# Batch 0's head in a four-batch chain of conditional layers: first expert piece by chunk, a new load order, and sums placed in other units

## What is computed

```python
def _gemma_mlp(x, gate_w, up_w, down_w):          # width 256 -> 1024 -> 256
    g = jnp.einsum('bsh,hi->bsi', x, gate_w)
    u = jnp.einsum('bsh,hi->bsi', x, up_w)
    return jnp.einsum('bsi,ih->bsh', jax.nn.gelu(g, approximate=True) * u, down_w)

x = x + top2_of_8_experts(x, softmax(cond)) + _gemma_mlp(x, shared...)       # L0
x = x + (silu(x @ W_up[e] + b_up[e]) * (x @ W_gate[e] + b_gate[e])) @ W_down[e] + b_down[e]   # L1, e = argmax(cond)
x = x + x @ sum_g(cond[g] * weight[g] * mask).T + bias                       # L2, masked
x = x + x @ W_base.T + b_base + 2 * sum_e cond[e] * (x @ As[e].T) @ Bs[e].T  # L3, rank 16
```

## Time and profile before

| what | value |
|---|---|
| median of 3 runs | 494.46 us (492.17 to 495.14) |
| the profiled execution | 492.72 us |
| its span, first to last instruction | 491.1 us |
| TensorE busy | 476.2 us, 97% |
| VectorE busy | 398.1 us, 81% |
| ScalarE busy | 274.6 us, 56% |
| GpSimd busy | 89.4 us, 18% |
| TensorE's granted clock | 1.00 throughout |

### The profile page before, as it was taken

The page is one execution under the profiler, slowest core; times in us unless marked ns, Lnnn a source line. Parts: engine busy times, 40 slices in busy tenths (PEclk is TensorE's granted clock), DMA queues, the critical chain, the costliest instruction groups (busy, mean ns, idle before and its releaser), DMA issues.

```text
span 491.1 us, 6836 instructions
## 1 busy us (share of the span) xinstructions
PE 476.2 (97%) x2166; PEld 393.8 (80%) x2166; DVE 398.1 (81%) x679; ACT 274.6 (56%) x448; POOL 89.4 (18%) x92
## 2 busy tenths in 40 slices
PE   8899888989999999999999999999999999999997
PEld 7688666768888888888888888888888888888886
DVE  7589988999878787578987979898887799974455
ACT  5556554666645565356654746675766356544432
POOL 1913239900009950100000020000000100000000
PEclk9999999999999999999999999999999999999999
DMA  6978773040931106872293016213039423000002
GB/s 173 204 223 249 142 113 116 1 128 29 194 115 41 32 5 135 179 209 75 70 171 81 1 48 188 77 53 111 20 86 185 118 64 102 28 1 1 0 1 85
DMA packets 112363, 47.33 MB, mean 96 GB/s; under 512 B 66424, under 2 KB 111096, under 8 KB 112328
## 3 DMA queue, kind: packets, MB, share of 16 engines
q1 hardware_dynamic: 109184, 41.30, 34.2%
q0 software_dynamic: 2560, 5.21, 4.3%
q10 hardware_dynamic: 584, 0.39, 0.3%
HBM read 44.79 MB, written 2.10 MB: 95 GB/s over the span
## 4 chain that ended last, share of the span: by engine, by line
PE 82%; DVE 8%; SPq 5%; DMA 3%; issue 1%; ACT 0%; ACTq 0%; DVEq 0%
PE bank_a L1671 7%; PE bank_b L1673 7%; PE bank_b L1671 7%; PE bank_a L1673 7%; PE bank_a L1672 7%; PE bank_b L1672 7%; PE tail L1695 4%; PE tail L1696 4%; PE tail L1699 4%; SPq L496 3%; PE out L1699 3%; PE out L1695 3%; PE out L1696 3%; PE bank_a L1938 2%; PE bank_a L1940 2%; PE bank_a L1939 2%
## 5 line engine op out<-in xcount | busy, mean ns | idle before, releaser
L713 ACT ACTIVATE hid_hi<-hid 128x512 fp32r<-128x512 f32 x84 | 53.1, 632 | 84.8 <-DVE hid L1006 53.8
L1014 DVE TENSOR_TENSOR hid_lo<-hid,hid_hi 128x512 fp32r<-128x512 f32 x84 | 61.9, 737 | 18.4 <-ACT hid_hi L713 18.4
L1006 DVE SCALAR_TENSOR_TENSOR hid<-bank_b,mine,hid 128x512 f32<-128x512 f32 x64 | 47.5, 742 | 27.8 <-PE bank_b L1673 26.7
L705 ACT ACTIVATE hid<-bank_a 128x512 f32<-128x512 f32 x68 | 40.4, 594 | 40.9 <-PE bank_a L1673 40.0
L995 DVE TENSOR_TENSOR res_lo<-raw,res_hi 128x768 fp32r<-128x768 f32 x36 | 36.1, 1004 | 1.1 <-ACT res_hi L692 1.1
L995 DVE TENSOR_TENSOR w_lo<-raw,w_hi 128x768 fp32r<-128x768 f32 x30 | 29.5, 984 | 2.8 <-ACT w_hi L692 2.8
L692 ACT ACTIVATE res_hi<-raw 128x768 fp32r<-128x768 f32 x36 | 30.2, 839 | 1.2 <-DMA raw<-in_L_cond_skill_down 1.2
L1671 PE MATMUL bank_a<-x_hi,res_hi 128*128 128x512 f32 x74 | 28.9, 390 | 0.0
L1672 PE MATMUL bank_a<-x_lo,res_hi 128*128 128x512 f32 x74 | 28.8, 390 | 0.0
L1673 PE MATMUL bank_a<-x_hi,res_lo 128*128 128x512 f32 x74 | 28.8, 389 | 0.0
L1671 PE MATMUL bank_b<-x_hi,res_hi 128*128 128x512 f32 x74 | 28.8, 389 | 0.0
(11 more groups left out here) (362 smaller groups left out, 1349.8 us busy)
## 6 DMA issues: line engine op xcount, KB each, us to landing
raw<-in_L_cond_skill_gate SPq DMA_DIRECT2D x32, 256.0 KB, 3.2
raw<-in_L_cond_skill_up SPq DMA_DIRECT2D x32, 256.0 KB, 3.4
raw<-in_L_cond_skill_down SPq DMA_DIRECT2D x64, 128.0 KB, 3.5
raw<-in_L_cond_shared_down SPq DMA_DIRECT2D x18, 128.0 KB, 3.7
early<-in_L_cond_weight POOLq DMA_DIRECT2D x2, 1024.0 KB, 7.1
raw<-in_L_cond_shared_gate SPq DMA_DIRECT2D x8, 256.0 KB, 3.4
raw<-in_L_cond_shared_up SPq DMA_DIRECT2D x8, 256.0 KB, 3.6
raw_gate<-in_L_cond_W_gate SPq DMA_DIRECT2D x16, 128.0 KB, 4.0
```

Of the source, the lines that this page charges most:

```text
L705: nc.scalar.activation(hid[:, tile_of(g)], bank_a[tile_of(g)][:, :], func, **kw).then_inc(act_ready, 1)
L713: nc.scalar.activation(hid_hi[:, tile_of(g)], hid[:, tile_of(g)], ACT.Copy).then_inc(hid_hi_ready, 1)
L1006: ins = nc.vector.scalar_tensor_tensor(tile, bank, weight, tile, ALU.mult, ALU.mult)
L1014: nc.vector.tensor_tensor(hid_lo[:, tile], hid[:, tile], hid_hi[:, tile].bitcast(F32), ALU.subtract).then_inc(hid_lo_ready, 1)
```

## The change

- Piece 1 (the first expert's first two chunks) is loaded by chunk: three transfers for a chunk (gate, up, down) on a semaphore of its own, six in all in place of four. ScalarE's `split` waits for the chunk alone. `take_chosen` moves ahead of `first_parts`' first subtraction.
- `PIECE_ORDER` of batch 0: joint pieces 2, 4 and 6 each one or two places earlier; L1's 12 transfers behind own piece 12, not 14.
- `first_combined`'s parts go from units 5, 7, 9, 10 to 2, 5, 7, 9; ScalarE's part of them from 8 and 9 to 6 and 8; `pair_main_hi` and `pair_sums` from 10 to 9, `pair_main_lo` from 11 to 10, c3's sum from 9 to 10 and its high part from 10 to 11.
- `bias_base` goes from joint unit 0 to batch 1's unit 1, `bias_lora` from there to unit 3.
- `share` becomes b3_t (256 columns), and `first_a2` multiplies and adds in halves of 256 columns: 14 pairs in place of 7 for each of the two batches. It waits for l3_f in place of base_sums.

```diff
--- before.py
+++ after.py
@@ -58,10 +58,10 @@
 L3_LO_AT = 8
 W2_AT = 8
 BIAS_LOADS_AT = 11
-T_AT = {5: 0, 7: 1, 9: 2, 10: 3}
-T_HI_AT = {8: ((0, 2), (2, 3)), 9: ((1, 4), (3, 5))}
-MAIN_AT = 10
-SUMS_AT = {0: 10, 2: 4}
+T_AT = {2: 0, 5: 1, 7: 2, 9: 3}
+T_HI_AT = {6: ((0, 2), (2, 3), (1, 4)), 8: ((3, 5),)}
+MAIN_AT = 9
+SUMS_AT = {0: 9, 2: 4}
 SUMS_LO_AT = {0: 11, 2: 5}
 
 C_PLACE = {0: 9, 1: 11, 2: 1, 3: 3}
@@ -75,7 +75,8 @@
 X2_SUM = {1: 5, 2: 5}
 X2_PLACE = {1: 5, 2: 4}
 XSUM_SECOND = 12
-BIAS_LORA_AT = 1
+BIAS_BASE_AT = 1
+BIAS_LORA_AT = 3
 BIAS_AT = 3
 L1_TURN = {13: 0, 14: 1, 15: 2, 16: 3}
 L1_TURN_LO = {14: 0, 15: 1, 16: 2, 17: 3}
@@ -146,7 +147,8 @@
     return (i - (SHARED if b < JOINT else 0)) // MLP_CHUNKS
 
 
-PIECE_ORDER = ([("own", 0, c) for c in range(0, 14, 2)] + [("joint", 0, 2), ("own", 0, 14), ("joint", 0, 4), ("own", 0, 16), ("joint", 0, 6)]
+PIECE_ORDER = ([("own", 0, c) for c in range(0, 10, 2)] + [("joint", 0, 2), ("own", 0, 10), ("own", 0, 12), ("joint", 0, 4), ("own", 0, 14),
+                ("joint", 0, 6), ("own", 0, 16)]
                + [("own", 1, c) for c in range(0, OWN[1], 2)]
                + [("own", 2, 0), ("own", 2, 2), ("own", 2, 4), ("joint", 2, 0), ("own", 2, 6), ("own", 2, 8), ("joint", 2, 2),
                   ("own", 2, 10), ("joint", 2, 4), ("own", 2, 12), ("joint", 2, 6), ("own", 2, 14)]
@@ -162,7 +164,7 @@
 
 
 def raw_landed(j):
-    return 64 * ((j - 1) // RAW_SLOTS + 1)
+    return 64 * ((j - 1) // RAW_SLOTS + (raw_slot(j) > 0))
 
 
 SLOTS = [[i % 4 if i < UNIT_AT[0] else i % 2 for i in range(OWN[0])],
@@ -230,6 +232,7 @@
         a3_lo = sb("a3_lo", [P, D], F32R)
         b3_raw = raw_down1[:, 1, :]
         b3_t = sb("b3_t", [P, D])
+        share = b3_t[:, :]
         b3_y = raw_up1[:, :, :].rearrange("p k h -> p (k h)")
         b3_y_hi = sb("b3_y_hi", [P, B * D], F32R)
         b3_y_lo = sb("b3_y_lo", [P, B * D], F32R)
@@ -243,7 +246,6 @@
         u3_work = raw_down1[:, 3, :]
         bias_all = sb("bias_all", [P, B, D])
         base_nat = sb("base_nat", [P, KD, D])[:, :, :]
-        share = base_nat.rearrange("p k d -> p (k d)")
         b3_nat = bias_all[:, 0, :].rearrange("p (k e r) -> p k e r", k=KD, e=E)
         bias2_again = bias_all[:, 1, :]
         b3_u3 = bias_all[:, 2, :].rearrange("p (k e r) -> p k e r", k=KD, e=E)
@@ -299,6 +301,7 @@
 
         raw_in = [sem(f"raw_in{s}") for s in range(RAW_SLOTS)]
         second_in = sem("second_in")
+        skill_in = [sem(f"skill_in{c}") for c in range(2)]
         first_down_in = [sem(f"first_down_in{c}") for c in range(2)]
         x0_in = [sem(f"x0_in{k}") for k in range(KD)]
         x_in = [None] + [sem(f"x_in{b}") for b in range(1, B)]
@@ -352,6 +355,7 @@
         xs_lo_ready = sem("xs_lo_ready")
         a2_step = sem("a2_step")
         a2_share = sem("a2_share")
+        a2_sum = sem("a2_sum")
         weights_f = sem("weights_f")
         weights_hi = sem("weights_hi")
         weights_lo = sem("weights_lo")
@@ -474,6 +478,8 @@
                         sp.wait_ge(pair_w_lo, PARTS * (PAIRED[b2] + c2 + 1 - FIRST_JOINT[b2]) + 2)
                 m = c if kind == "joint" or (b < JOINT and c < SHARED) else (c - (SHARED if b < JOINT else 0)) % MLP_CHUNKS
                 cols = slice(m * P, (m + 2) * P)
+                if j == 1:
+                    return load_by_chunk(slot, m, gate, up, down)
                 for n, w in ((0, gate), (2, up)):
                     sp.dma_start(raw[:, slot, n:n + 2, :],
                                  w.rearrange("(k p) i -> p k i", p=P)[:, :, cols]).then_inc(raw_in[slot], 16)
@@ -481,6 +487,15 @@
                     sp.dma_start(raw[:, slot, 4:6, half_n * P:(half_n + 1) * P],
                                  down[(m + half_n) * P:(m + half_n + 1) * P, :]
                                  .rearrange("p (j d) -> p j d", j=KD)).then_inc(raw_in[slot], 16)
+
+            def load_by_chunk(slot, m, gate, up, down):
+
+                for c in range(2):
+                    place, rows = slice(c * P, (c + 1) * P), slice((m + c) * P, (m + c + 1) * P)
+                    for n, w in ((0, gate), (2, up)):
+                        sp.dma_start(raw[:, slot, n:n + 2, place],
+                                     w.rearrange("(k p) i -> p k i", p=P)[:, :, rows]).then_inc(skill_in[c], 16)
+                    sp.dma_start(raw[:, slot, 4:6, place], down[rows, :].rearrange("p (j d) -> p j d", j=KD)).then_inc(skill_in[c], 16)
 
             shared = [t["L0_cond_shared_" + n] for n in ("gate", "up", "down")]
             skill = [t["L0_cond_skill_" + n] for n in ("gate", "up", "down")]
@@ -548,7 +563,7 @@
                 load_piece(j, *(rows if kind == "own" and own_skill >= 0 else shared))
                 if (kind, b, c) == ("own", 0, 4):
                     load_x(1)
-                if (kind, b, c) == ("own", 0, 14):
+                if (kind, b, c) == ("own", 0, 12):
                     for n in range(3):
                         first_l1(n)
                 if (kind, b, c) == ("own", 1, 2):
@@ -609,17 +624,20 @@
             def first_a2(b):
 
                 if b == 0:
-                    pool.wait_ge(base_sums, KD)
+                    pool.wait_ge(l3_f, 1)
                     pool.wait_ge(w2_in, 48)
                     pool.wait_ge(tail_free, len(PREPS))
                 else:
                     pool.wait_ge(weights_lo, 3 * b - 1)
                 nc.gpsimd.tensor_scalar(a2[:, :], w2_raw[:, 0, :], picks[:, b, 5:6], None, ALU.mult).then_inc(a2_step, 1)
                 for n in range(1, E):
-                    pool.wait_ge(a2_step, b * A_STEPS + n)
-                    nc.gpsimd.tensor_scalar(share, w2_raw[:, n, :], picks[:, b, 5 + n:6 + n], None, ALU.mult).then_inc(a2_share, 1)
-                    pool.wait_ge(a2_share, b * (E - 1) + n)
-                    nc.gpsimd.tensor_tensor(a2[:, :], a2[:, :], share, ALU.add).then_inc(a2_step, 1)
+                    for k in range(KD):
+                        part, done = slice(k * D, (k + 1) * D), b * (E - 1) + n - 1
+                        pool.wait_ge(a2_step, b * A_STEPS + n)
+                        wait(pool, a2_sum, done + k)
+                        nc.gpsimd.tensor_scalar(share, w2_raw[:, n, part], picks[:, b, 5 + n:6 + n], None, ALU.mult).then_inc(a2_share, 1)
+                        pool.wait_ge(a2_share, KD * done + k + 1)
+                        nc.gpsimd.tensor_tensor(a2[:, part], a2[:, part], share, ALU.add).then_inc((a2_sum, a2_step)[k], 1)
                 pool.wait_ge(a2_step, b * A_STEPS + E)
                 nc.gpsimd.tensor_tensor(a2[:, :], a2[:, :], mask_nat[:, :], ALU.mult).then_inc(a2_step, 1)
                 pool.wait_ge(a2_step, b * A_STEPS + E + 1)
@@ -673,7 +691,10 @@
         def _(act):
             def split(b, i):
                 j = piece_of("own", b, i)
-                act.wait_ge(raw_in[raw_slot(j)], raw_landed(j))
+                if j == 1:
+                    act.wait_ge(skill_in[i % 2], 48)
+                else:
+                    act.wait_ge(raw_in[raw_slot(j)], raw_landed(j))
                 earlier = slot_before(b, i)
                 if earlier is not None:
                     act.wait_ge(down_done, downs_done(*earlier))
@@ -881,12 +902,12 @@
                         l3_operand_hi()
                     if i in T_HI_AT:
                         combined_hi(0, T_HI_AT[i])
-                    if i == C_PLACE[0] + 1:
-                        weights_split_hi(c3_hi, c3[:, :], (weights_f, 1))
                     if i == MAIN_AT:
                         pair_main_hi(0, 0)
                     if i == SUMS_AT[0] + 1:
                         pair_sums_hi(0, 0)
+                    if i == SUMS_LO_AT[0]:
+                        weights_split_hi(c3_hi, c3[:, :], (weights_f, 1))
 
             def second():
                 b = 1
@@ -1338,6 +1359,8 @@
                         x_turn_blocks(1)
                     if i == X1_LO_AT:
                         later_x_lo(1)
+                    if i in T_AT:
+                        first_combined(T_AT[i])
                     if i == L3_TURN_AT:
                         l3_turn_blocks()
                     if i == L3_OPERAND_AT:
@@ -1345,17 +1368,13 @@
                         l3_operand()
                     if i == L3_LO_AT:
                         l3_operand_lo()
-                    if i in T_AT:
-                        first_combined(T_AT[i])
-                    if i == C_PLACE[0]:
-                        c3_sum(0)
                     if i == SUMS_AT[0]:
                         pair_sums(0, 0)
                     if i == MAIN_AT + 1:
                         pair_main_lo(0, 0)
+                        c3_sum(0)
                     if i == SUMS_LO_AT[0]:
                         pair_sums_lo(0, 0)
-                    if i == C_PLACE[0] + 2:
                         weights_split_lo(0, 1, c3_hi, c3_lo, c3[:, :])
 
             def first_combined(part):
@@ -1407,6 +1426,8 @@
                         residual_lo(b, 1)
```

(7 more changed lines are left out.)

## The result

| | before | after |
|---|---|---|
| median (lowest to highest), 15 runs each | 493.56 us (491.04 to 496.32) | 489.75 us (488.53 to 493.25) |
| ratio, 95% interval | | 0.9932 (0.991 to 0.9955) |
| the profiled execution, its span | 492.72, 491.1 us | 492.13, 490.2 us |

The change is worth 3.8 us (0.8%; by the ratio, 3.4 us), where I had forecast 7.0; so it falls under "within 1%". The profiled execution of the changed kernel is one of its longer ones. The first experiment therefore profiled the same kernel again.

The account below looks back on a forecast made before the run. TensorE is full from 120 us on, so only its earlier waits, 10.6 us at most, can go. 2.0 + 1.9 + 1.5 + 0.6 + 1.5 - 0.5 = 7.0 us, from 494.46 to 487.5 us; range 484.2 to 491.2.

Parts of the forecast that it names:

- Part 1 (A): 2.3 us TensorE wait at 13.6 us for the first expert's first weights; loading by chunk takes away 2.0 us.
- F: 1.9 us TensorE wait on L1533 at 98.6 us; kept as it is in the forecast.
- Part 2 (B): 1.9 us wait at 57.7 us for joint unit 0's low part; spreading the sums takes it all away.
- Part 3 (C): 1.6 us wait at 69.8 us for VectorE's sum; moving bias_base out of joint unit 0 gains 1.5 us.
- Part 4 (D, F): GpSimd's sum in halves, started sooner: holds of 0.55 us, not 1.1; 0.6 us gained, 0.5 us subtracted for longer overlap.
- D: 1.2 us TensorE wait at 73.2 us for VectorE's hid_lo, held by GpSimd; 0.6 us taken as gone.
- Part 5 (E): 1.5 us wait at 77.9 us on ScalarE's copy; joint piece 4 issued near 61 us removes it, 3 us slack.
- VectorE gives it back: Rival, chance 0.20: joint units 1 to 4 become VectorE-bound through holding, giving back 3.5 us; 491.0.
- joint piece 4 is still late: Rival, chance 0.10: L1's 12 transfers need 24 us beside GpSimd's loads; about 1.5 us of wait stays; 489.0.
- slower case through long holds: Rival, chance 0.05: halves hold VectorE as long as wholes in joint units 0 to 3; TensorE waits 10 us more; 497.
- three signs of being wrong: Two-input VectorE instructions held 1.1 us; SyncE's L1 issues past 65 us; hid_lo or L1533 waits summing over 4 us.

Follow-up runs that it names:

- after_again: The changed kernel, unaltered, timed and profiled again beside the kernel before: 489.23 us, ratio 0.992.
- l1_up_behind_joint4: The changed kernel with the last four of L1's 12 transfers issued behind joint piece 4, not in front of it: 487.84 us, ratio 0.9893.
- the base: The changed kernel with the last four of L1's 12 transfers issued behind own piece 14: 487.19 us, ratio 0.9864.
- the four of the second group: Against the base: a2's additions made one-input multiplications 485.49, batch 0's a2 in wholes 487.08, a2 from joint unit 4 487.03, bias_base in joint unit 0 488.29 us.
- whole_sums: The base with a2 of batch 0 summed in wholes of 512 columns on another, more coarsely rounded tile: 487.08 us, ratio 0.9889.
- sums_as_before: The base with block sums, weight sums, joint weights' parts and c3 in the units of the kernel before: 489.58 us, ratio 0.9917.
- piece1_whole: The base with piece 1 loaded whole again by four transfers, take_chosen still early: 488.02 us, ratio 0.9885.
- c0_at_10: The base with the product that needs b3_y_lo one unit later, in unit 10: 486.17 us, ratio 0.9855.
- one_input_adds: The base with GpSimd's a2 additions replaced by one-input multiplications, leaving out the sum over eight weights: 485.49 us, ratio 0.9845.
- best: c0_at_10 plus batch 0's a2 from joint unit 4, its split in batch 1's unit 2, bias columns' stores before batch 1's a2: 483.50 us, ratio 0.9792.
- order_as_before: The changed kernel with PIECE_ORDER and the place of L1's transfers as in the kernel before: 493.51 us, ratio 0.9999.

## Why the prediction was half right

**Part 1 (A): right in its place, wrong in what it is worth.** The third transfer was issued at 8.33 us in after_again (forecast 8.4), ScalarE had its data by 11.1 (11.9), TensorE began unit 2 at 13.42 (13.8): 2.4 us sooner than before. The failed sentence is "whatever TensorE gains before that moves the whole rest forward by as much". It holds only where VectorE isn't the bound, and the rows that I had read said it was: 9.96 of 10 us busy from 40 to 50 us, beside a full TensorE. The other failed sentence is "I cost the later pieces at nothing". VectorE's timeline of after_again:

```profile
27.42 0.96 DVE L1016 TENSOR_TENSOR w_lo<-raw,w_hi 128x768 fp32r<-128x768 f32 x1 [1.30 <-ACT w_hi L713]
...
46.74 1.22 DVE L1304 TENSOR_TENSOR b_y_lo<-raw_up,b_y_hi 128x1024 fp32r<-128x1024 f32 x1
```

At 27.4 us VectorE had stood idle for 1.30 us, because ScalarE had waited 2.5 us for the next piece to land; from there to 50 us it has no pause of over 0.4 us. So b3_y_lo comes at 46.74 where it was 46.48 before, although TensorE started unit 2 2.4 us earlier. Seven profiles have this same head without slow first products (after_again, l1_up_behind_joint4, the base and the four of the second group). The split that waits for this landing starts at 26.38 to 28.12 us in them, b3_y_lo 19.0 to 19.3 us behind it in each, and at 50 us TensorE is 1.80 us (earliest landing, whole_sums) to 0.06 us (latest, the base) ahead of the kernel before. So the landing and VectorE's list behind it set this place, and what is left of A differs from execution to execution. With the sums in their old units (sums_as_before) the same stretch of VectorE takes 18.2 us, b3_y_lo comes at 45.39, and 1.8 of A's 1.9 us are still there at 50 us. Parts 1 and 2, which my sum added as if they were independent, share one list. The same cover hides bad luck too: in the first profile TensorE started 2.1 us late, and 0.8 of it is left at 50 us (0.30 against -0.46). Of A's 2.0 us, by piece1_whole, 0 to 1.4 us (its profile beside two others) reach the end, by the medians 0.8, within noise. For B to F together the table gives 4.2 us in after_again, from 50 us on.

**Part 2 (B): right, but the walk was too short at its tightest place.** The wait on L1485 is gone, the table shows 2.2 us between 50 and 60 us, and sums_as_before gives back 2.3 us. "0.7 us later and just fits" for b3_y_lo was wrong: TensorE waits 0.5 to 0.6 us for it in nearly every profile, and c0_at_10 shows that this costs 0.8 us. The walk started from VectorE's state in the kernel before; with TensorE sooner by A, the product that wants b3_y_lo comes sooner as well. I had moved the supply and not the demand.

**Part 3 (C): right.** No wait at L1533's place in the first profile, 0.6 in the second; putting bias_base back brings 1.4 us of wait and takes 1.5 us of gain between 50 and 100 us. Batch 1 took it in at no cost, as said.

**Part 4 (D, F): the mechanism and the size of a hold right, the price of the overlap too low.** Additions of 128x256 take 0.74 us (forecast 739 ns) and hold VectorE by 0.54 us (forecast 0.55); D's wait is 0.42 of 1.2 (I took 0.6 as gone). The start was at 63.9 us (62), the end at 102.3 (95): GpSimd's multiplications take 1363 ns on the mean, and up to 2.3 us, while VectorE is busy. This brought the still whole multiplication by the mask into the stretch where TensorE is ahead, a hold of 1.1 us at 99.8 us in the first profile (hid_lo, 1.53 us of wait) and at 103 us in the second. I had priced the longer overlap at 0.5 us. In after_again F did go in its old place (1.9 us more by 100 us in the table) and came back as 0.6 + 2.4 us over the next two units. For all holds together one_input_adds gives 2.6 us of waits and 3.6 us by its profile from 50 us on, `best` beside c0_at_10 2.7 us of median. The Trainium skill (GPSIMD Engine Reference, Performance versus the Vector engine) puts an addition at 2.6 cycles a column, which I had estimated as 1.11 us for 512 columns: that is the hold of a whole here, 1.1 us, and half of it, 0.54, that of a half, while the instructions themselves take 1.29 and 0.74 us. That holds are as long in sum whichever way they are cut was what my rival "VectorE gives it back" rested on, and whole_sums agrees with it (6.7 us of holds against 7.4).

**Part 5 (E): the step that failed first.** I let the 12 transfers start at 43 us and run 18.3 us, as before; they started at 46.05 and ran 21.3 us, 45.28 and 20.2 us in the second profile. So piece 4 went out at 67.3 and 65.5 us, not at 61, and the "3 us of slack" were gone. This is the rival "joint piece 4 is still late", whose time I had given as 489.0. It too was priced too low, since it saw no clock: in the first profile the stretch from 76 to 85 us cost 4.0 us, where the second gained 1.2. Whether GpSimd's 2 MB of loads beside them made the transfers slow, as that rival had it, wasn't tried; in order_as_before, back in their old place, they ran 19.6 us (53.64 to 73.23), so the place alone doesn't explain the length. The new order is still the most valuable part: 4.3 us by order_as_before, since a late piece 4 takes whatever B, C and D give.

**In sum.** Forecast 7.0; by the traces of after_again 4.7, by medians 3.8. A's 2.0 are somewhere from 0 to 1.4, E's 1.5 are between -4.0 and +1.2, b3_y_lo costs 0.8, and the holds 2.6 to 3.6. That 489.75 us lies in the stated range is owed to the range's width, not to the sum: it lies outside the 486.5 to 488.5 of the forecast itself, beside the 489.0 of the rival that had a chance of 0.10. The 487.5 was also made from a median of 494.46; from the 493.56 of the 15 runs it would have been 486.6. Of the three signs of being wrong that I had named, two came: SyncE's L1 issues ran past 65 us (to 67.30 and 65.47), and a subtraction of VectorE was still held by 1.1 us, by the multiplication by the mask. The third didn't: the waits on hid_lo and on L1533's successor sum to 2.6 and 3.3 us. TensorE wasn't full from 105 us on in the second profile either. That a slower case through long holds (497) didn't come is in line with 0.54 us by a half: I had put the turning point at 0.9. What stays open is where the unprofiled runs lost their time: 24 runs of the changed kernel lie between 488.3 and 493.3 us, 17 of them with a granted clock below 0.998, and only two were profiled, one of each kind.

## What to carry to other kernels

A gain of TensorE counts only where the engine that supplies it isn't full as well. Follow a moved start to the next full window of VectorE or the next landing before adding it to a sum. A queue that is moved forward moves its long issues forward in front of everything behind it, so count the queue's own time from its own start, and put what is wanted first in front. When several waits are taken away ahead of one that depends on a load, that one can take all of the gain; move it first. And one profile is one execution: before two are compared, look at where each stands among its kernel's runs, and compare what they gain between two places, not where they end.
